# Sums of exponentials halved on GpSimd, and query and key projections in three 16-bit products, in the two narrow attentions

## The reference

```python
q = (query @ Wq.T + bq).reshape(B, S, H, dh).transpose(0, 2, 1, 3)
k = (key @ Wk.T + bk).reshape(B, S, H, dh).transpose(0, 2, 1, 3)
v = (value @ Wv.T + bv).reshape(B, S, H, dh).transpose(0, 2, 1, 3)
scores = jnp.einsum('bhqd,bhkd->bhqk', q, k) / SCALE
scores = scores + chemical_bias[:, None, :, :]         # layer 1 alone
scores = jnp.where(mask == 0, -jnp.inf, scores)        # layer 1 alone
attn = jax.nn.softmax(scores, axis=-1)
out = jnp.einsum('bhqk,bhkd->bhqd', attn, v)
x = x + out.transpose(0, 2, 1, 3).reshape(B, S, D) @ Wo.T + bo
```

## Time and profile before

| what | us |
|---|---|
| median of 3 runs | 1663.77 (1658.26 to 1664.56) |
| the profiled execution's own time | 1670.5 |
| its span, first to last instruction | 1668.7 |
| masked layer: first projection to last addition to x | 821.9 to 1070.5 |
| unmasked layer | 1400.1 to 1599.4 |
| TensorE busy over the span | 1416.6 (85%) |
| VectorE / ScalarE / GpSimd busy | 951.9 / 891.1 / 782.9 |

### The profile page before, as it was taken

The page is one execution under the profiler, slowest core; times in us unless marked ns, Lnnn a source line. Parts: engine busy times, 40 slices in busy tenths (PEclk is TensorE's granted clock), DMA queues, the critical chain, the costliest instruction groups (busy, mean ns, idle before and its releaser), DMA issues.

```text
span 1668.7 us, 36916 instructions
## 1 busy us (share of the span) xinstructions
PE 1416.6 (85%) x14429; PEld 876.3 (53%) x14522; DVE 951.9 (57%) x1964; ACT 891.1 (53%) x1455; POOL 782.9 (47%) x690
## 2 busy tenths in 40 slices
PE   3999999997399999999599898669494995999948
PEld 2466666665267777777444343335372553444425
DVE  4566566665344444444488888654756234666653
ACT  2667776663189999999354444212132222555512
POOL 5577776663279999999532232010502003444200
PEclk9999999998599999999899999769695997999968
DMA  7000000000400000000100100000000000000000
GB/s 253 8 8 8 7 8 8 2 2 5 144 14 26 25 25 25 25 25 14 61 29 30 58 29 26 1 0 0 27 3 1 1 0 10 8 8 5 2 1 26
DMA packets 25637, 39.95 MB, mean 24 GB/s; under 512 B 6884, under 2 KB 12937, under 8 KB 24873
## 3 DMA queue, kind: packets, MB, share of 16 engines
q1 hardware_dynamic: 24936, 36.10, 6.7%
q0 software_dynamic: 576, 2.10, 0.6%
HBM read 39.24 MB, written 1.05 MB: 24 GB/s over the span
## 4 chain that ended last, share of the span: by engine, by line
PE 68%; DVE 15%; issue 10%; POOL 2%; ACT 2%; SPq 1%; DMA 1%; POOLq 0%; DVEq 0%; ACTq 0%
PE bank L2056 10%; PE bank L2044 10%; PE bank L1345 4%; DVE sbuf L1455 4%; PE bank L1698 3%; PE bank L2257 3%; PE bank L1283 3%; PE bank L1770 3%; PE bank L1751 2%; PE bank L1721 2%; DVE sbuf L1472 2%; PE bank L2243 2%; PE bank L1791 2%; PE bank L1702 2%; DVE sbuf L320 2%
## 5 line engine op out<-in xcount | busy, mean ns | idle before, releaser
L2027 POOL TENSOR_TENSOR sbuf<-sbuf 128x512 f16<-128x512 f32 x256 | 307.3, 1210 | 63.4 <-ACT sbuf L2082 61.7
L2082 ACT ACTIVATE sbuf<-bank,sbuf 128x512 f32<-128x512 f32 (+1 forms) x512 | 317.2, 698 | 15.8 <-PE bank L2044 6.4
L2056 PEld LDWEIGHTS bank<-sbuf 128*128 128x128 f16 x3072 | 192.7, 98 | 59.5
L2056 PE MATMUL bank<-sbuf 128*128 128x128 f16 x3072 | 212.7, 219 | 0.0
L2044 PE MATMUL bank<-sbuf 128*128 128x512 f16 x768 | 208.6, 382 | 2.9 <-DVE sbuf L2094 2.9
L1455 DVE TENSOR_REDUCE sbuf<-bank 128x4 f32<-128x1024 f32 x128 | 156.4, 1222 | 76.5 <-PE bank L1299 65.7
L326 POOL TENSOR_TENSOR sbuf<-sbuf 128x16 f32<-128x16 f32 x8 | 23.3, 2908 | 375.8 <-DVE sbuf L316 375.8
L1668 POOL TENSOR_TENSOR sbuf<-sbuf 128x512 f16<-128x512 f32 x128 | 148.5, 1181 | 79.8 <-ACT sbuf L1850 79.8
L2104 DVE SCALAR_TENSOR_TENSOR sbuf<-bank,sbuf 128x128 f32<-128x128 f32 x256 | 71.9, 343 | 189.7 <-PE bank L2056 189.7
L1252 POOL TENSOR_TENSOR sbuf<-sbuf 128x512 f16<-128x512 f32 x64 | 66.5, 1040 | 239.0 <-ACT sbuf L1397 239.0
L1345 PE MATMUL bank<-sbuf 128*32 128x256 f32 x2048 | 138.5, 389 | 1.6 <-ACT sbuf L1417 1.6
(11 more groups left out here) (235 smaller groups left out, 2712.9 us busy)
## 6 DMA issues: line engine op xcount, KB each, us to landing
sbuf<-w SPq DMA_DIRECT2D x32, 256.0 KB, 2.7
sbuf<-bias_t SPq DMA_DIRECT2D x4, 1024.0 KB, 15.9
sbuf<-ctx_t SPq DMA_DIRECT2D x24, 128.0 KB, 2.7
sbuf<-bias_q POOLq DMA_DIRECT2D x4, 512.0 KB, 14.9
sbuf<-mask_t SPq DMA_DIRECT2D x8, 256.0 KB, 2.7
sbuf<-bias_t SPq DMA_DIRECT2D x8, 256.0 KB, 3.0
sbuf<-mask_q SPq DMA_DIRECT2D x8, 256.0 KB, 3.6
sbuf<-bias_q SPq DMA_DIRECT2D x8, 256.0 KB, 4.3
```

Source lines behind the costliest of these rows:

```text
L2027: g.tensor_tensor(hid16[1][:, u % BUFS, :], hid[:, u % 4, :], hid16[0][:, u % BUFS, :], ALU.subtract)\
L2056: last = pe.matmul(bank[4 + out_no % 2][:, j * P:(j + 1) * P], hid16[h][:, u % BUFS, j * P:(j + 1) * P], w2_16[p][:, w, f * D:(f + 1) * D] ...
L2082: last = act.activation(to, bank[u % 4][:, :], ACT.Gelu, bias=b1[u // U][:, u % FT0:u % FT0 + 1], scale=1 / SCALE)
```

## The change

In both narrow attentions:

- GpSimd adds, for each pair, the exponentials of the two key tiles (`halves`, 128 x 512 float32, L1284 in the new kernel), and part 1 of `mix` runs over this sum: 4 matmuls (L1379) in place of 8. It waits for `halves`.
- Weights and activations of the query and key projections are split into a high and a low 16-bit part, the weights scaled by 256. A projection is 6 float16 matmuls of 128 x 256 (high by high, high by low, low by high, for two output tiles; L1318) in place of 2 float32 ones; ScalarE takes the 256 out again.
- VectorE splits the weights once per layer, 4 instructions of 128 x 512. GpSimd splits the activations, `operands`, once per batch: 2 casts and 2 subtractions of 128 x 256 (L1260 to L1264).
- GpSimd's program interleaves these with the splits: per pair `halves(u)`, at n = 0 to 3 then a split of the next batch, and at n = 6 then the operands of the batch after the next.

```diff
@@ -1188,6 +1191,10 @@
+            wq16, wk16 = (take([2, HG, P], F16) for _ in range(2))
+            xs16, cs16 = ([take([2, S], F16) for _ in range(2)] for _ in range(2))
+            PASSES = ((0, 0), (0, 1), (1, 0))
+            SCALE = 2.0 ** 8
+            both = take([EXPS, HW])
...
+                def operands(b):
+                    g.wait_ge(ctx_in[b % 2], b // 2 * 16 + 16)
+                    wait(g, s["projected"], (b - 1) * JOBS)
+                    xt = xn_t[:, b * S:b * S + S]
+                    g.tensor_copy(cs16[b % 2][:, 0, :], ctx_t[b % 2])
+                    g.tensor_copy(xs16[b % 2][:, 0, :], xt).then_inc(s["operands"], 1)
+                    g.wait_ge(s["operands"], 2 * b + 1)
+                    g.tensor_tensor(cs16[b % 2][:, 1, :], ctx_t[b % 2], cs16[b % 2][:, 0, :], ALU.subtract)
+                    g.tensor_tensor(xs16[b % 2][:, 1, :], xt, xs16[b % 2][:, 0, :], ALU.subtract).then_inc(s["operands"], 1)
+
...
-                for b in range(B):
-                    for k in range(QK):
-                        split_(b, k)
+                def halves(u):
+
+                    g.wait_ge(s["exps"], u + 1)
+                    if u >= EXPS:
+                        g.wait_ge(s["mixed"], 2 * (u // 2 - 1))
+                    e = exps[:, u % EXPS, :].rearrange("p (j m c) -> p j m c", j=2, c=S)
+                    g.tensor_tensor(both[:, u % EXPS, :].rearrange("p (j c) -> p j c", c=S), e[:, :, 0, :], e[:, :, 1, :],
+                                    ALU.add).then_inc(s["halves"], 1)
+
+                g.wait_ge(nrm_xt, normed)
+                operands(0)
+                for k in range(QK):
+                    split_(0, k)
+                operands(1)
+                for u in range(B * PER_BATCH):
+                    b, n = divmod(u, PER_BATCH)
+                    halves(u)
+                    if b + 1 < B and n < QK:
+                        split_(b + 1, n)
+                    if b + 2 < B and n == PER_BATCH - 2:
+                        operands(b + 2)
...
             def tensor(pe):
                 pe.wait_ge(far_in, 16 * FAR_LOADS)
-                pe.wait_ge(nrm_xt, normed)
+                pe.wait_ge(s["weights"], 2)
...
                     if k == 0:
-                        pe.wait_ge(ctx_in[b % 2], b // 2 * 16 + 16)
+                        pe.wait_ge(s["operands"], 2 * b + 2)
...
                     if k < QK:
                         pair, kind = divmod(k, 2)
-                        for c in range(2):
-                            last = pe.matmul(to[:, c * S:(c + 1) * S], (wq, wk0)[kind][:, 2 * pair + c, :],
-                                             ct if kind else xt, start=True, stop=True)
+                        for c, (n, (w, a)) in product(range(2), enumerate(PASSES)):
+                            last = pe.matmul(to[:, c * S:(c + 1) * S], (wq16, wk16)[kind][:, w, 2 * pair + c, :],
+                                             (xs16, cs16)[kind][b % 2][:, a, :], start=n == 0, stop=n == 2)
...
-                    for m in range(SB):
+                    if part:
+                        pe.wait_ge(s["halves"], 2 * Q + 2)
                         for j in range(HG):
-                            at = g * HG * 32 + 32 * j
-                            lhs = tens[:, g, :] if part else val[b % 2][:, m, at:at + 32]
-                            at = (j % 2) * HW + m * S
-                            last = pe.matmul(bank[O_BANK[b % 2]][32 * j:32 * j + 32, part * S:part * S + S], lhs,
-                                             exps[:, (2 * Q + j // 2) % EXPS, at:at + S], start=g == part == m == 0,
-                                             stop=g == GROUPS - 1 and m == SB - 1, skip_group_check=True)
+                            at = (j % 2) * S
+                            last = pe.matmul(bank[O_BANK[b % 2]][32 * j:32 * j + 32, S:2 * S], tens[:, g, :],
+                                             both[:, (2 * Q + j // 2) % EXPS, at:at + S], start=False,
+                                             stop=g == GROUPS - 1, skip_group_check=True)
+                    else:
+                        for m in range(SB):
+                            for j in range(HG):
+                                at = g * HG * 32 + 32 * j
+                                lhs = val[b % 2][:, m, at:at + 32]
+                                at = (j % 2) * HW + m * S
+                                last = pe.matmul(bank[O_BANK[b % 2]][32 * j:32 * j + 32, 0:S], lhs,
+                                                 exps[:, (2 * Q + j // 2) % EXPS, at:at + S], start=g == m == 0,
+                                                 stop=g == GROUPS - 1 and m == SB - 1, skip_group_check=True)
                     last.then_inc(s["mixed"], 1)
...
                             last = act.activation(x32[:, k % 2, c * S:(c + 1) * S], src[:, c * S:(c + 1) * S], ACT.Identity,
-                                                  bias=bias, scale=DH ** -0.5 if kind == 0 else 1.0)
+                                                  bias=bias, scale=(DH ** -0.5 if kind == 0 else 1.0) / SCALE)
...
             def vector(v):
                 c = dve(v)
                 v.wait_ge(far_in, 16 * FAR_LOADS)
+                for w, to in ((wq, wq16), (wk0, wk16)):
+                    c.step(v.tensor_scalar(to[:, 0], w, SCALE, None, ALU.mult)).settle()
+                    v.scalar_tensor_tensor(to[:, 1], w, SCALE, to[:, 0], ALU.mult, ALU.subtract).then_inc(s["weights"], 1)
```

More of the change, by code:

```diff
@@ L1158, in narrow_attention @@
             s = {k: sem(L + k) for k in (
+                "weights",
+                "operands",
                 "projected",
@@ L1170, in narrow_attention @@
                 "exps",
+                "halves",
                 "mixed",
@@ L1275, in project @@
                     if k == 0:
-                        pe.wait_ge(ctx_in[b % 2], b // 2 * 16 + 16)
+                        pe.wait_ge(s["operands"], 2 * b + 2)
                     to = job_bank(b, k)
-                    xt = xn_t[:, b * S:b * S + S]
                     ct = ctx_t[b % 2]
```

## The result

The changed kernel takes 1738.37 us in the median (1736.49 to 1739.84, 4 runs), against 1664.16 (1658.26 to 1673.47, 4 runs) for the kernel before: 1.0433 times as long, with a 95% interval of 1.0403 to 1.0463. The forecast was 1692, its range 1648 to 1712. The direction was right, and the time lies 26 us above the range. The profiled execution took 1739.84, with a span of 1738.0 against 1668.7.

The account below looks back on a forecast made before the run. TensorE bounds the unmasked layer, TensorE and VectorE nearly fill the masked one. Seven batches x (3.0 + 0.6) = 25, plus 2 x 2.0 = 29 us on 1670.5, so 1.017, or 1692 on the median; range 1648 to 1712.

Parts of the forecast that it names:

- What TensorE saves: Both layers: part 1 of mix 0.57 us, saving 0.43; projection 0.70, saving 0.36; each 4 times a batch, together 3.1.
- `halves`: GpSimd's addition of 128 x 512 takes 1.15 us, with 1.48 as the upper bound.
- The holds: GpSimd's additions and splits hold VectorE's cut, its lines near 0.7 us in the mean; masked batch +3.0, unmasked +0.6.
- Rivals 1 and 2: Cut's holds stay off the path, 1633 us, chance 0.12; or it is held only once, 1670 us, chance 0.17.
- The heads: At each layer's start the first projection waits for the operands of batch 0: +2.0 us a layer.
- rival 3: As forecast, plus clock falls in the masked layer: one 3.4 us stretch a batch, +12, time 1704, chance 0.13.
- The row with 2.19 busy ahead of a fall: Masked layer's last batch before the change: TensorE busy 2.19 of 3.40 us at 1048.5, clock at 0.50 from 1053.4.
- A last batch at no change: Each layer's last batch has no splits and no operands, so it was counted at no change.

Follow-up runs that it names:

- filler: The changed kernel with 8 idle 16-bit matmuls that nobody reads on TensorE ahead of each maxima: 1723.96 us, ratio 1.0385.
- The larger number of idle matmuls: The changed kernel with 8 idle matmuls ahead of each maxima, and 4, 8 and 4 behind weigh of masked pairs 0, 4 and 6: 1718.82 us, 1.0284.
- `halves` alone: The changed kernel with float32 projections back, without operands or split weights; additions and halved part 1 stay: 1714.63, 1721.10, 1743.67 and 1744.30 us.

## Why the prediction was right in kind and wrong in size

- **What TensorE saves**: right. Part 1 takes 0.57 as forecast (1014.78 to 15.35). The projection takes 0.77 (15.35 to 16.12) and not 0.70, within its bounds.
- **`halves`**: 1.27 instead of 1.15, between the bounds.
- **The holds**: right in mechanism, place and size. The cut's lines have means of 0.65 and 0.75 (forecast 0.7; before they were 0.36 and 0.30, and not the 0.18 and 0.19 of the single rows). A batch at the full clock takes 31.93 and 23.29 with filler (forecast 32.3 and 23.4). Rivals 1 and 2 fall. The kernel before plus additions has nearly the same holds (means of 0.52 and 0.73) with all of TensorE's work, and batches of 32.97 (clock 0.97) and 23.45; by 1.0065 against 1.0299 it is the additions' place and not their number that costs most. GpSimd does wait in turn too, as L1284's 1.52 shows.
- **The heads**: +5.7 for 4, 3.8 in the masked and 1.8 in the unmasked layer.
- **The step that failed is the clock**: the sum of the forecast has no term for it, and rival 3 ("one a batch gives +12"), with a chance of 0.13, had it too small, and with it the upper end of the range. I priced it as one stretch of 3.4 us, in the masked layer only, and took the falls for rare. In the trace a masked batch has at least one fall, most of 6.8 us and some of 13.7 or 17.1, and the unmasked layer and both last batches have them too. Taking 7 x (2.6 + 0.5) for the holds at the full clock from the filler run and 5.7 for the heads, 27.4 of the table's 68.9 us are explained and 41.5 are left. Of these, 5.4 lie in the unchanged code between the layers, and 36 in the layers, where rival 3 had 12. The 36 go with 167 more us at 1.2 GHz, 0.2 of a microsecond each in the mean. That such time costs is shown by batches of the same instructions (23.77 and 28.04, 28.93 and 33.36, 22.98 and 30.13), and there it is 0.3 to 0.5 for each; that it is all of the 36 isn't shown. The row with 2.19 busy ahead of a fall couldn't have told me how often the clock would fall, since in the kernel before six masked batches have as little and no fall.
- **A last batch at no change** was wrong as well, +6.7 and +8.5. The additions alone, with TensorE's work as before, give +3.7 and +2.0 there; the rest comes with a lower clock (0.68 and 0.55), which isn't shown to be its cause.

What stays open: how the 36 us divide between the clock and holds that meet worse once the engines are out of step. The larger number of idle matmuls brings back 25 us, not all of it surely by the clock, and costs time itself. The fall sets in at other places from one run to the next, which may be why `halves` alone ran from 1715 to 1744.

## What to carry to other kernels

Work moved to an idle engine isn't free if it holds up another. Look for the short VectorE instruction on the path, here the cut, and ask what starts just ahead of it on GpSimd. Waits that set this order were worth 2.6% here (1.0433 to 1.0173), and 1% where GpSimd had no additions (1.0021 to 0.9922). And where TensorE is some 85% busy, both a stall and a saving can go with a lower clock: price a wait not by its length alone but by the stretch at half speed that may follow it, here 3.4 to 17.1 us, and test a free saving by itself before you count on it.

## What was not expected of the hardware

- A GpSimd instruction that only writes holds a VectorE TENSOR_SCALAR of 8 numbers a partition for 1.00 to 1.34 us instead of 0.18 in most cases; a split and the memset behind it together hold it for up to 2.20.
- With four float32 matmuls less per part 1 more time is at 1.2 GHz (37.2 us in the masked layer for 9.2), and the program gets no faster. With idle matmuls less time is, and with the larger number of them the changed kernel is 1.5% faster (1.0284 for 1.0433).
- GpSimd's addition of 128x512 takes 1.27 us with two float32 inputs and a float32 result (L1284), and 1.15 with one 16-bit input and a 16-bit result (L1274).
